# Attention, layers and dispatch of a fused network, from two stages to one written-out stage of 78 beats

## The chip, the cores and the metric

One core of a Trainium2 chip (trn2) runs the whole network in one launch. The metric is the device time of that launch in microseconds (us); less is better. The engines are TensorE (PE, with its weight loads shown as PEld), VectorE (DVE), ScalarE (ACT), GpSimd (POOL) and the DMA queues, which SyncE (SP) mostly feeds.

## The reference, cut to what matters

Input and output are 8 images of 128 channels and 32x32 pixels, 8192 tokens of 128 numbers in all, in float32. Three residual steps follow each other:

```python
x = x + _L0_conv_ref(_gn(x), ...)              # group norm, deformable convolution
t = _to_tokens(x)
t = t + _L1_attn_ref(_ln_t(t), ...)            # token norm, attention layer
t = t + _L1_ffn_ref(_ln_t(t), ...)             # token norm, top-2 of 8 experts
```

The second one is what the change touches, with the router of the third:

```python
res = _local_rel_attention(x, ...)             # 8 heads, 65 keys around each token, bias by distance
xs = _layer_norm(x + res, ln1_g, ln1_b)
res = relu(xs @ W_lin + b_lin)
xs = _layer_norm(xs + res, ln2_g, ln2_b)       # added to t
logits = xt @ Wr + br                          # xt: the normed tokens; softmax, top 2, weights
```

Every token then goes to its two experts; their weighted sum is added to t.

## The kernel before, in words

Tokens lie as channels by tokens: `X` holds the residual stream, `XA` the normed tokens with 32 zero columns at either end of an image. A **half** is half an image, 512 tokens or four **tiles** of 128; there are 16. `program` calls stages, each a block of its own with a barrier behind it: `front` and `sample_fast` (convolution), `token_norm`, `attention`, `finish` (layers and dispatch), `experts`, `combine`. In each block every engine has its own written list, and semaphores order them.

**`attention`** works in 64 units of 128 tokens, four to a half; a Fori loop (L1187) holds four halves and runs three times, so it returns twice; the two halves before it and the two behind it are written out. For a unit: PE's `scores` (L1304, 32 small matmuls into `p_s`, four banks), DVE's `soft` (L1480 adds scaled scores and bias table, L1486 the row maximum), ACT's `exps` (L1407, eight heads), PE's `turn` (L1317, eight transposes into `p_t`), `copy_pt` (ACT L1415, DVE L1493), PE's `mix` (L1331, weights by values into `p_o`), DVE's `scale` (reciprocal L1501, multiply L1503), PE's `turn_out` (L1340) and ACT's `copy_out` (L1419). PE's body of unit t is, in order:

```python
scores(t + 1); turn_out(t - 2); product; turn(t); product; mix(t - 1)
```

The products make queries and keys (L1273), values (L1279) and the output projection (L1284) a half at a time through one bank, `p_m`; ACT or DVE drains each (L1401, L1458, L1464, L1471), and the next waits for that. DVE also copies `XA` into a ring `XS` for the values (L1449). SP moves the values' windows (12 transfers a half).

**`finish`** starts behind attention's barrier and goes over the halves in steps of a skewed pipeline: centering 1 (PE L1747), square (ACT L1800), variance 1 (L1756), inverse root (ACT Ln and Exp L1792, L1794), DVE's multiply L1972, the linear layer (L1738), ReLU (ACT L1833), residual (DVE L1965), centering 2 (L1762), variance 2 (L1732), DVE L1957 and L1961 (sum into `X`). Their PSUM banks are the stage's own. Halves then go in groups to dispatch (half 0, six pairs, the last three one by one): transposes (L1706), router matmuls (L1714), DVE's statistics (`note`, L1861 to L1869) and choice (`choose`, L1876 to L1903), counts by PE (L1721, L1722), DVE's `place_rows` (L1910 to L1950), the normed rows by ACT (L1813), and POOL's indirect DMAs that write each tile's rows twice to the experts' table in DRAM (L1690, behind a counter step L1686). At the end DVE makes the table of blocks (L1989 to L2018) and folds the experts' input scale into `w1` (L2023), and SP writes the padding rows.

Of the kernel before, what the change touches and what calls it, by code (L numbers as in the profile page):

```python
# [14 lines left out]
ALU = mybir.AluOpType  # L15
# [31 lines left out]
PADS = EXPERTS + SPARE  # L47
ROW = P + 4
# [878 lines left out]

class MidWeights:
# [16 lines left out]
    MID, EXP = 16 * 10, 16 * 6  # L945
# [12 lines left out]
def token_norm(nc, d, X, XA, const, mid, ew):  # L958
# [4 lines left out]
    with ExitStack() as st:  # L963
# [11 lines left out]
        written = sem(nc, st, "n_written")  # L975

        with nc.Block() as block:
            @block.sync
            def _(sp):
                for dst, src in ((center, "c_center"), (ones, "c_ones"), (const.ident, "c_ident")):  # L980
                    sp.dma_start(dst[:], d[src]).then_inc(w_in, 16)

# [5 lines left out]
                for dst, src in ((ew.w1, "w1"), (ew.w2, "w2"), (ew.lng, "ln_g"), (ew.lnb, "ln_b"), (ew.b1, "b1")):  # L988
                    sp.dma_start(dst[:], d[src]).then_inc(mid.experts_in, 16)
# [59 lines left out]
def attention(nc, d, XA, const):  # L1049
# [7 lines left out]
    PADA = PIX + 2 * REACH  # L1057
    VW = DV + 1
    NU = TOK // (UB * QB)
    NS = 2 * IMAGES  # L1060
    US = NU // NS
    NB = US * UB
    NT = HEADS
    NPM = 1
    COPIES = 12
    with ExitStack() as st:
        ident = const.ident
        wq = sb(nc, st, "a_wq", [P, 2, P])
        wk = sb(nc, st, "a_wk", [P, 2, P])
        wv = sb(nc, st, "a_wv", [P, P])  # L1070
        wo = sb(nc, st, "a_wo", [P, P])
        bq = sb(nc, st, "a_bq", [P, 2])
        bk = sb(nc, st, "a_bk", [P, 2])
        bv = sb(nc, st, "a_bv", [P, P])
        bo = sb(nc, st, "a_bo", [P, 1])


        bias = [sb(nc, st, f"a_bias{v}", [P, 4, 2, QW]) for v in range(3)]
        XS = [sb(nc, st, f"a_XS{j}", [P, CH]) for j in range(2)]
        Q = [sb(nc, st, f"a_Q{j}", [P, 2, CH]) for j in range(2)]  # L1080
        KT = [sb(nc, st, f"a_KT{j}", [P, 2, PADA]) for j in range(2)]

        VT = [sb(nc, st, f"a_VT{j}", [P, TPC, HEADS, VW]) for j in range(2)]
        V = sb(nc, st, "a_V", [QW, 2 * NB, HEADS, VW])
        E = [sb(nc, st, f"a_E{b}", [P, NT, QW]) for b in range(2)]
        PT = [sb(nc, st, f"a_PT{b}", [QW, NT, P]) for b in range(2)]
        nm = sb(nc, st, "a_nm", [P, 2, NT])
        rsum = sb(nc, st, "a_rsum", [P, 2, HEADS])
        O = [sb(nc, st, f"a_O{b}", [P, P]) for b in range(2)]
        OT = [sb(nc, st, f"a_OT{j}", [P, CH]) for j in range(2)]  # L1090

        p_s = ps(nc, st, "a_ps", (P, 4, CH))
        p_t = ps(nc, st, "a_pt", (P, 2, NT // 2, P))
        p_m = [ps(nc, st, f"a_pm{k}") for k in range(NPM)]
        p_o = ps(nc, st, "a_po")
        toeplitz = nc.dram_tensor("toeplitz", [QB, 4, 2, QW], F32, kind="Internal").ap()

        w_in = sem(nc, st, "a_w_in")
        rel_in = sem(nc, st, "a_rel_in")
        masked = sem(nc, st, "a_masked")  # L1100
        cleared = sem(nc, st, "a_cleared")
        staged = sem(nc, st, "a_staged")
        windowed = sem(nc, st, "a_windowed")
        made = sem(nc, st, "a_made")
        act_took = sem(nc, st, "a_act_took")
        dve_took = sem(nc, st, "a_dve_took")
# [1275 lines left out]
```

## Time and profile before

| | us |
|---|---|
| runs of the kernel | 1542.88, 1550.11, 1549.81 (median 1549.81) |
| the profiled execution: span | 1543.9 |
| front and sampling, 0 to 543.7 | 543.7 |
| token norm, 543.7 to 597.4 | 53.7 |
| attention, 597.4 to 991.4 | 394.0 |
| layers and dispatch, 991.4 to 1218.1 | 226.7 |
| experts and combine, 1218.1 to the end | 325.8 |

The profiled execution is one of its own; what is known of its time is its span, from the first to the last instruction. Over that span PE is busy 1234.7 us, PE's weight loads 794.5, DVE 980.6, ACT 777.2 and POOL 607.0; the mean granted clock of PE is 0.889 of full speed. The stage bounds are the first instructions behind each barrier. These totals mix stages with different limits: the stage views further down tell more than they do. In a row of a timeline stand the start, the duration, the engine, the line, the operation with what it writes and reads, how many instructions the row holds, and in brackets the idle time before it and what ended it.

### The profile page before, as it was taken

The page shows a single profiled execution, that of the slowest core. Times are in us where ns is not written, and L with a number is a line of the kernel's source. Part 1 is how long each engine was busy: PE and PEld are TensorE (multiplying, and loading weights), DVE is VectorE, ACT ScalarE, POOL GpSimd, SP SyncE. Part 2 cuts the span into 40 slices and gives each one's busy share as a digit, 9 for nine tenths or more (in the row PEclk, how much of TensorE's full clock was granted, in tenths as well). Part 3 has the DMA queues.
Part 4 walks back from the last instruction along what each step waited for, and adds up shares of the span by engine and source line. Part 5 has one row for each costly group of instructions (what it writes and reads, how often), then busy time and mean ns, then how long its engine had stood idle before and what let it go on. Part 6 is the DMA issues. An engine that isn't in the chain of part 4 may idle for free. (4 is left out here: it accounts for less than half of the span.)

```text
span 1543.9 us, 42335 instructions
## 1 busy us (share of the span) xinstructions
PE 1234.7 (80%) x13479; PEld 794.5 (51%) x13480; DVE 980.6 (64%) x2321; ACT 777.2 (50%) x2037; POOL 607.0 (39%) x681
## 2 busy tenths in 40 slices
PE   3981799999999965788888788787865399999974
PEld 1551344444444421455555555433334399999962
DVE  4996888888888511566566566467765244444435
ACT  1212545555455243456565555467752277777750
POOL 2000577878778800000000000015777455656550
PEclk9995899999999987799899999698865699999985
DMA  3000000000000030111211211101111122222228
GB/s 120 0 0 12 1 1 1 0 0 0 0 0 0 1 138 27 45 36 35 46 40 31 46 44 36 57 9 37 54 51 63 44 68 67 69 67 67 69 68 306
DMA packets 69491, 67.75 MB, mean 44 GB/s; under 512 B 13151, under 2 KB 59231, under 8 KB 68983
## 3 DMA queue, kind: packets, MB, share of 16 engines
q1 hardware_dynamic: 58615, 44.23, 10.5%
q0 software_dynamic: 8448, 17.58, 3.4%
q10 hardware_dynamic: 2304, 4.20, 0.7%
q8 instruction: 90, 1.47, 0.4%
q14 instruction: 34, 0.28, 0.1%
HBM read 29.93 MB, written 23.00 MB: 34 GB/s over the span
## 5 line engine op out<-in xcount | busy, mean ns | idle before, releaser
L2157 ACT ACTIVATE e_hT<-e_ph,e_b 128x128 f32<-128x128 f32 x544 | 155.0, 368 | 73.7 <-PE e_ph L2114 68.5
L1407 ACT ACTIVATE a_E<-a_E,a_nm 128x96 f32<-128x96 f32 x512 | 142.7, 362 | 72.1 <-DVE a_nm L1486 72.0
L440 POOL TENSOR_TENSOR s_pc<-s_wide,VP 128x512 f32<-128x512 f32 x112 | 143.1, 1278 | 74.7 <-ACT s_wide L519 68.6
L673 PE MATMUL s_pbc<-s_AT,s_sel 120*128 120x512 bf16 x400 | 134.5, 386 | 32.8 <-ACT s_wide L519 17.5
L431 POOL TENSOR_TENSOR s_acc<-s_acc,s_pb 128x512 f32<-128x512 f32 x112 | 142.3, 1270 | 22.0 <-DVE s_pb L602 21.5
L684 PE MATMUL s_pout<-s_pa,s_opT 128*128 128x512 f32 x288 | 150.8, 605 | 0.0
L2125 PE MATMUL e_py<-e_w,e_hT 128*128 x1088 | 149.3, 280 | 1.3 <-ACT e_hT L2157 0.8
L1674 POOL MEMSET m_total<- 128x8 f32 x1 | 0.1, 109 | 378.5 <-POOLq L1193 378.5
L2114 PE MATMUL e_ph<-e_xT,e_w1s 128*128 128x128 f32 x1088 | 147.3, 279 | 0.3 <-DVE e_w1s L2186 0.2
L1690 POOL DMA_INDIRECT slots<-m_pay,m_pos x128 | 129.2, 1009 | 38.5 <-issue 37.6
L2095 POOL DMA_INDIRECT picks<-e_yw,e_rows x136 | 134.6, 990 | 22.6 <-POOL e_tick L2093 18.5
L2114 PEld LDWEIGHTS e_ph<-e_xT,e_w1s 128*128 128x128 f32 x1088 | 133.8, 194 | 2.0 <-issue 1.0
L2125 PEld LDWEIGHTS e_py<-e_w,e_hT 128*128 128x128 f32 x1088 | 131.8, 191 | 4.6 <-issue 3.0
L519 ACT ACTIVATE s_wide<-s_pbc 128x512 f32<-128x512 f32 x112 | 66.4, 593 | 115.7 <-PE s_pbc L673 113.7
L602 DVE TENSOR_TENSOR s_pb<-s_pbc,VP 128x512 f32<-128x512 f32 x144 | 98.1, 681 | 27.8 <-PE s_pbc L673 27.8
L689 PE MATMUL s_pout<-s_pc,s_opT 128*128 128x512 f32 x224 | 114.4, 592 | 0.0
L673 PEld LDWEIGHTS s_pbc<-s_AT,s_sel 120*128 120x128 bf16 x400 | 38.4, 98 | 132.3 <-issue 56.7
L602 DVE TENSOR_TENSOR s_pa<-s_pbc,VP 128x512 f32<-128x512 f32 x144 | 98.3, 683 | 12.4 <-PE s_pbc L673 11.8
L2186 DVE COPY e_w1s<-e_w 128x512 f32 x136 | 59.0, 434 | 67.6 <-issue 67.6
L1304 PE MATMUL a_ps<-a_KT,a_Q 32*32 32x96 f32 x4096 | 67.5, 262 | 30.6 <-issue 27.2
L1480 DVE SCALAR_TENSOR_TENSOR a_E<-a_ps,a_bias 128x768 f32<-128x768 f32 x64 | 61.1, 955 | 45.1 <-PE a_ps L1304 44.6
L2192 DVE TENSOR_TENSOR e_yb<-e_py,e_b 128x128 f32<-128x128 f32 x136 | 39.6, 291 | 74.3 <-PE e_py L2125 74.0
(221 smaller groups left out, 2426.9 us busy)
## 6 DMA issues: line engine op xcount, KB each, us to landing
a_V<-a_VT SPq DMA_DIRECT2D x176, 68.0 KB
e_rows<-slots SPq DMA_DIRECT2D x136, 66.0 KB, 1.8
c_y<-picks SPq DMA_DIRECT2D x16, 512.0 KB, 6.1
X<-in_x SPq DMA_DIRECT2D x8, 512.0 KB, 8.5
e_w<-in_w SPq DMA_DIRECT2D x2, 2048.0 KB, 10.1
out<-c_o ACTq DMA_DIRECT2D x16, 256.0 KB
picks<-e_yw,e_rows POOLq DMA_INDIRECT x136, 2.3
slots<-m_pay,m_pos POOLq DMA_INDIRECT x128, 2.3
```

The costliest lines, as they stand in the source:

```text
L431: nc.gpsimd.tensor_tensor(acc[j][:], before, prod_b[b % 3][:], ALU.add)\
L440: nc.gpsimd.tensor_tensor(prod_c[k][:].rearrange("p (a b) -> p a b", a=HALF), wide[k][:].rearrange("p (a b) -> p a b", a=HALF), window(n, ...
L602: dve.tensor_tensor(out[:].rearrange("p (a b) -> p a b", a=HALF), p_bc[bank_of["spread", t]][:].rearrange("p (a b) -> p a b", a=HALF), win ...
L673: pe.matmul(p_bc[bank_of["spread", t]][:], sel[:, t % 5, :], AT[j][:, t // 5, :], start=True, stop=True).then_inc(bc, 1)
L684: pe.matmul(p_out[j][:], opT[:], prod_a[a % 3][:], start=(a == 0), stop=False)\
L689: pe.matmul(p_out[j][:], opT[:], prod_c[(j * NC + i) % 2][:], start=False, stop=False)\
L1407: act.activation(E[u % 2][:, o, :], E[u % 2][:, o, :], ACT.Exp, bias=nm[:, u % 2, o:o + 1]).then_inc(powered, 1)
L1690: nc.gpsimd.indirect_dma_start(out=slots, out_offset=bass.IndirectOffsetOnAxis(ap=pos[h][:, c, t:t + 1].bitcast(U32), axis=0), in_=pay[c][ ...
L2095: nc.gpsimd.indirect_dma_start(out=picks, out_offset=bass.IndirectOffsetOnAxis(ap=rows[j][:, P:P + 1].bitcast(U32), axis=0), in_=yw[j][:], ...
L2114: last = pe.matmul(p_h[j % 2][:, q * P:(q + 1) * P], w1s[j % 2][:, q, :], xT[j % 2][:], start=True, stop=True)
L2125: last = pe.matmul(p_y[j % 2][:, 0:P], hT[j % 2][:, q, :], w2[:, bass.ds(e, 1), q * P:(q + 1) * P].rearrange("p o h -> p (o h)"), start=(q ...
L2157: ins = act.activation(hT[j % 2][:, q, :], p_h[j % 2][:, q * P:(q + 1) * P], ACT.Gelu, bias=b1[:, bass.ds(e, 1), q:q + 1].rearrange("p o h ...
```

## The change

`attention` and `finish` become one function, `middle`, with one block and no loop: 78 **beats** (64 units and 14 more), all written out. The weights and the bias table of attention are loaded in `token_norm`'s block. A beat t is a unit as before, with one step of the layers of some half put in behind `turn`. Half h has its centering 1 in beat t = 7 + 4h, variance 1 one beat later, then the linear layer, centering 2, variance 2, the sum into `X`, the transposes (beat + 6) and the router (beat + 8); so each beat works at one to three of them. Their results go into the score banks `p_s`, as PSUM has no others: the layer matmul waits until DVE has read the scores (`biased`), and the next scores wait until ACT or DVE has read the layer's result (`emptied`). ACT does its layer step between the fourth and fifth exponential, and the inverse roots behind its copy. What DVE multiplied in L1957 and L1972, and the normed rows that ACT made, POOL makes now. Groups of halves are as before (0; 1 and 2; ... 11 and 12; 13; 14; 15); the dispatch of one is spread over five to eight beats, and of the last three over fewer. The ring `XS` and its copies go; `w2` of the experts shares its memory with the keys, and loads when the last scores are done. The padding rows go from DRAM to DRAM. The matmuls that fold the experts' bias move from behind the last half into beat 68. The new functions of PE, POOL and DVE are, in the diff cut to its core:

```diff
+def middle(nc, d, X, XA, const, aw, mid, ew, table, slots):
...
+    C1, V1, LIN, C2, V2, ADD, TURN, JUDGE = 0, 1, 2, 3, 4, 5, 6, 8
+    BEATS = NU + 14
...
+                sp.wait_ge(scored, NU)
+                sp.dma_start(ew.w2, d["w2"]).then_inc(w2_in, 16)
...
+                def rows(g, first):
...
+                        nc.gpsimd.tensor_scalar(pay[0][h][:, k, 0:P], pay[0][h][:, k, 0:P], inv[h][:, 1, k:k + 1],
+                                                nb[h][:, k:k + 1], ALU.mult, ALU.add).then_inc(paid, 1)
...
+                for t in range(BEATS):
+                    h = at(t, LIN)
+                    if h is not None:
+                        pool.wait_ge(inverted1, h * 2 + 2)
+                        pool.wait_ge(kept1, h + 1)
+                        if h:
+                            pool.wait_ge(added, h)
+                        nc.gpsimd.tensor_tensor(xs[:], c1g[:], sq1[:], ALU.mult).then_inc(scaled1, 1)
+                    h = at(t, ADD)
+                    if h is not None:
+                        pool.wait_ge(inverted2, h * 2 + 2)
+                        pool.wait_ge(kept2, h + 1)
+                        if h:
+                            pool.wait_ge(finished, h)
+                        nc.gpsimd.tensor_tensor(z[:], c2g[:], sq2[:], ALU.mult).then_inc(scaled2, 1)
+                    g = group_at(t, ORDER)
+                    if g is not None:
+                        rows(g, 0)
+                    g = group_at(t, COUNT)
+                    if g is not None and tiles(g) > TPC:
+                        rows(g, TPC)
+                    for part in range(4):
+                        g = group_at(t - part, WRITE)
+                        if g is not None and PARTS[g][-1] < NS - 3:
+                            send(g, part, 4)
+                    g = group_at(t, WRITE)
+                    if g is not None and PARTS[g][-1] >= NS - 3:
+                        send(g, 0, 1)
...
+                def emptied(t):
+                    h = at(t, C1)
+                    if h is not None:
+                        pe.wait_ge(kept1, h + 1)
+                    h = at(t, V1)
+                    if h is not None:
+                        pe.wait_ge(inverted1, h * 2 + 1)
...
+                def scores(t):
...
+                    if t:
+                        pe.wait_ge(biased, t)
+                    emptied(t - 2)
...
+                def layers(t):
+                    if t + 1 < NU:
+                        pe.wait_ge(biased, t + 2)
+                    else:
+                        emptied(t - 1)
+                    h = at(t, V1)
+                    if h is not None:
+                        pe.wait_ge(squared1, h + 1)
+                        pe.matmul(p_s[:, 0], ones[:], sq1[:], start=True, stop=True).then_inc(varied1, 1)
+                    h = at(t, LIN)
+                    if h is not None:
+                        pe.wait_ge(scaled1, h + 1)
+                        pe.matmul(p_s[:, 0], lin[:], xs[:], start=True, stop=True).then_inc(layered, 1)
...
+                for t in range(BEATS):
+                    if t + 1 < NU:
+                        scores(t + 1)
+                    if 0 <= t - 2 < NU:
+                        turn_out(t - 2)
+                    for x in due(t)[:1]:
+                        product(x)
+                    if t < NU:
+                        turn(t)
+                    layers(t)
+                    for x in due(t)[1:]:
+                        product(x)
+                    if 0 <= t - 1 < NU:
+                        mix(t - 1)
+                    if t == NU + 4:
...
+                        exps(t + 1, 0, HEADS // 2)
+                    layers(t)
+                    if t + 1 < NU:
+                        exps(t + 1, HEADS // 2, HEADS)
+                    if t < NU:
+                        copy_pt(t)
+                    roots(t)
...
+                    if t + 1 < NU:
+                        soft(t + 1)
...
+                    if 0 <= t - 1 < NU:
+                        scale(t - 1)
+                    g = group_at(t, PLACE)
+                    if g is not None:
+                        place(g)
+                    g = group_at(t, CHOOSE)
                     if g is not None:
                         choose(g)
+                    g = group_at(t, ORDER)
                     if g is not None:
+                        mark(g)
...
-            attention(nc, d, XA, const)
...
-            finish(nc, d, X, XA, const, mid, ew, table, slots)
+            middle(nc, d, X, XA, const, aw, mid, ew, table, slots)
```

Three places of the programs' order follow, without time. The names: `a_` are tiles and semaphores of attention, `l_` of the layers, `m_` of dispatch; `e_shared` holds the keys in the changed kernel.

**PE, in the layers and dispatch stage of the kernel before**: one step and the start of the next, with a group's counts and the first transposes of the next group.

```order
L1738 MATMUL l_pl<-l_xs0,l_lin 128x512 [waits l_clipped,l_scaled0]
L1721 MATMUL m_pr<-m_both,m_upper 128x32 [waits m_route]
L1722 MATMUL m_pr<-m_both,m_full 128x32
L1747 MATMUL l_pc10<-XA,k_center 128x512 [waits l_scaled0]
L1756 MATMUL l_pv<-l_sq11,k_ones 128x512 [waits l_inverted1,l_inverted0,l_squared0]
L1762 MATMUL l_pc2<-l_y1,k_center 128x512 [waits l_scaled1,l_added]
L1706 MATMUL m_pt0<-k_ident,X 128x128 [waits m_paid,l_finished]
L1706 MATMUL m_pt0<-k_ident,X 128x128 x3
L1706 MATMUL m_pt1<-k_ident,X 128x128 x4
L1714 MATMUL m_pr<-m_wrc,X 128x8 [waits m_route]
```

Layer matmuls wait for layer and dispatch results alone and write banks of that stage. **PE in the changed kernel, in the stage of units**: the last beat of a half, from the output's transpose to the next scores.

```order
L1526 MATMUL a_po<-k_ident,a_O1 128x128 [waits a_ostored,a_scaled]
L1499 MATMUL a_pt<-k_ident,a_E1 96x128 [waits a_pt_dve,a_powered]
L1499 MATMUL a_pt<-k_ident,a_E1 96x128 [waits a_powered] x3
L1499 MATMUL a_pt<-k_ident,a_E1 96x128 [waits a_pt_act,a_powered]
L1499 MATMUL a_pt<-k_ident,a_E1 96x128 [waits a_powered] x3
L1555 MATMUL a_ps<-XA,k_center 128x512 [waits a_dve_took,a_biased]
L1559 MATMUL a_ps<-l_sq2,k_ones 128x512 [waits l_squared2]
L1564 MATMUL a_ps<-m_wrc,X 128x8 [waits l_finished]
L1564 MATMUL a_ps<-m_wrc,X 128x8 x3
L1517 MATMUL a_po<-a_V,a_PT0 32x17 [waits a_ostored,a_scaled,a_windowed1,a_pt_act,a_pt_dve]
L1517 MATMUL a_po<-a_V,a_PT0 32x17 x31
L1486 MATMUL a_ps<-e_shared,a_Q0 32x96 [waits l_inverted2,m_fetched,l_kept1,a_biased]
```

The centering of one half (L1555), the variance (L1559) and the router (L1564) of earlier ones stand now between a unit's transposes (L1499) and its mix (L1517), and write the banks of the scores; the scores that follow (L1486) wait for four semaphores, three of them of the layers and dispatch.

**DVE, at the end of a group's placing, before**: behind it come the next group's statistics and four layer steps.

```order
L1939 TENSOR_REDUCE m_fpos<-m_wpos 128x8 [waits m_route]
L1944 COPY m_pay<-m_dest 128x8 [waits m_sent0]
L1944 COPY m_pay<-m_dest 128x8
L1946 COPY m_pay<-m_sm 128x8
L1947 TENSOR_TENSOR m_pay<-m_sm,m_ex 128x8
L1950 CAST m_pos<-m_fpos 128x16 [waits m_route]
L1861 BN_STATS m_stats<-m_pt 128x6 [waits m_turned]
L1861 BN_STATS m_stats<-m_pt 128x6 x3
L1861 BN_STATS m_stats<-m_pt 128x6 [waits m_turned]
L1861 BN_STATS m_stats<-m_pt 128x6 x3
L1957 SCALAR_TENSOR_TENSOR l_z<-l_pc,l_vec,l_sq 128x512 [waits l_inverted1]
L1961 SCALAR_TENSOR_TENSOR X<-l_z,l_vec,X 128x512 [waits l_scaled1]
```

The bias step is not in this list: attention's DVE list was over. **DVE in the changed kernel, the same place**: the end of placing (L1901 to L1912) and what follows.

```order
L1901 TENSOR_REDUCE m_fpos<-m_wpos 128x8 [waits m_route]
L1906 COPY m_pay<-m_dest 128x8 x2
L1908 COPY m_pay<-m_sm 128x8
L1909 TENSOR_TENSOR m_pay<-m_sm,m_ex 128x8
L1912 CAST m_pos<-m_fpos 128x16 [waits m_route]
L1762 SCALAR_TENSOR_TENSOR a_E<-a_ps,a_bias 128x768 [waits a_turned,a_scored]
L1768 TENSOR_REDUCE a_nm<-a_E 128x8 [waits a_biased]
L1799 SCALAR_TENSOR_TENSOR X<-l_z,l_vec,X 128x512 [waits l_scaled2]
L1775 COPY a_PT<-a_pt 96x512 [waits a_mixed,a_turned]
L1742 TENSOR_SCALAR e_shared<-a_pm,a_bk 128x512 [waits a_made]
L1783 RECIPROCAL a_rsum<-a_po 128x8 [waits a_oturned,a_mixed]
L1785 TENSOR_TENSOR a_O<-a_po,a_rsum 128x128 [waits a_scaled]
```

The bias step of the next unit's scores (L1762) now stands right behind the placing, and what waits for the scores' banks stands behind both. Two of the layer steps are gone from DVE's list.

**POOL, at the end of dispatch, before**: the last groups' transfers and the end of its list.

```order
L1690 DMA slots<-m_pay,m_pos 67584x132 x16
L1686 TENSOR_TENSOR m_tick<-m_tick 1x1 [waits m_paid,m_labelled,m_ticked]
L1690 DMA slots<-m_pay,m_pos 67584x132 x16
L1686 TENSOR_TENSOR m_tick<-m_tick 1x1 [waits m_paid,m_labelled,m_ticked]
L1690 DMA slots<-m_pay,m_pos 67584x132 x8
L1656 UNCONDITIONAL_BRANCH [waits m_sent1,m_sent0]
```

The list then only waits for the transfers to land. **POOL in the changed kernel**, ahead of the last three groups: a half's second multiply, the first four of a group's 16 transfers, a half's first multiply, and the first two row scalings of the next group.

```order
L1405 TENSOR_TENSOR l_z<-l_c2g,l_sq 128x512 [waits l_finished,l_kept2,l_inverted2]
L1382 TENSOR_TENSOR m_tick<-m_tick 1x1 [waits m_paid,m_labelled,m_ticked]
L1386 DMA slots<-m_pay,m_pos 67584x132 x4
L1398 TENSOR_TENSOR l_xs<-l_c1g,l_sq 128x512 [waits l_added,l_kept1,l_inverted1]
L1370 TENSOR_SCALAR m_pay<-m_pay,m_inv,m_nb 128x128 [waits m_sent1,m_rooted,m_shifted]
L1372 TENSOR_SCALAR m_pay<-m_pay,m_inv,m_nb 128x128
```

Multiplies (L1398, L1405) and row scalings (L1370, L1372) now stand between transfers in one list, and a group's 16 transfers come as one part of four in a beat and the rest behind the next work.

## Rows read from the trace of the kernel before

**Rows 1.** Windows: us; busy PE, PEld, DVE, ACT, POOL (instructions); clock; DMA; GB/s.

```profile
624.00:991.40 367.40, 304.80 (x9036) 206.05 (x9036) 233.69 (x394) 207.70 (x670) 0.00 (x0) 0.91 0.17 38
991.40:1218.10 226.70, 146.26 (x456) 80.12 (x456) 136.52 (x730) 118.87 (x268) 131.73 (x143) 0.73 0.15 48
```

**Rows 2.** Timeline, one attention beat with two products.

```profile
802.98 1.12 PE L1284 MATMUL a_pm<-a_OT,a_wo 128*128 128x512 f32 x2
...
804.04 0.74 PE L1331 MATMUL a_po<-a_V,a_PT 96*32 96x17 f32 x64
...
804.76 1.04 PE L1304 MATMUL a_ps<-a_KT,a_Q 32*32 32x96 f32 x64
...
805.79 0.29 DVE L1503 TENSOR_TENSOR a_O<-a_po,a_rsum 128x128 f32<-128x128 f32 x1
806.01 0.96 DVE L1480 SCALAR_TENSOR_TENSOR a_E<-a_ps,a_bias 128x768 f32<-128x768 f32 x1
...
806.13 0.33 PE L1340 MATMUL a_po<-k_ident,a_O 128*128 128x128 f32 x1 [0.33 <-DVE a_O L1503]
...
806.33 1.34 PE L1317 MATMUL a_pt<-k_ident,a_E 128*96 128x128 f32 x8
...
807.99 2.23 ACT L1407 ACTIVATE a_E<-a_E,a_nm 128x96 f32<-128x96 f32 x8 [1.21 <-DVE a_nm L1486]
```

**Rows 3.** Waits, 620 to 985: us in all, times, longest.

```profile
DVE a_E L1480 <- PE a_ps L1304: 44.6, 39, 4.4
...
PE a_ps L1304 <- issue: 27.2, 17, 3.9
```

**Rows 4.** Timeline, attention's first product, and bias steps of units 9 and 64.

```profile
603.61 2.07 PE L1273 MATMUL a_pm<-XA,a_wq 128*128 128x512 f32 x2 [8.69 <-DMA a_bv<-in_bv]
...
667.58 0.96 DVE L1480 SCALAR_TENSOR_TENSOR a_E<-a_ps,a_bias 128x768 f32<-128x768 f32 x1
...
978.61 0.96 DVE L1480 SCALAR_TENSOR_TENSOR a_E<-a_ps,a_bias 128x768 f32<-128x768 f32 x1 [0.52 <-PE a_ps L1304]
```

**Rows 5.** Timeline, a layer step on DVE and on ACT.

```profile
1008.72 0.75 DVE L1965 SCALAR_TENSOR_TENSOR l_y<-l_y,l_vec,l_xs 128x512 f32<-128x512 f32 x1 [1.94 <-ACT l_y L1833]
1008.86 0.60 ACT L1800 ACTIVATE l_sq<-l_pc 128x512 f32<-128x512 f32 x1 [0.17 <-PE l_pc L1747]
...
1009.72 0.69 ACT L1792 ACTIVATE l_sq<-l_pv,k_eps 128x512 f32<-128x512 f32 x1 [0.26 <-PE l_pv L1756]
```

**Rows 6.** Timeline, DVE, dispatch of eight tiles: placing, statistics, choosing, marking.

```profile
1091.76 0.16 DVE L1914 TENSOR_SCALAR m_sm<-m_ex 128x8 f32<-128x8 f32 x1
...
1095.45 1.67 DVE L1861 BATCH_NORM_STATS2 m_stats<-m_pt 128x6 f32<-128x128 f32 x8
1097.15 0.64 DVE L1865 BATCH_NORM_AGGREGATE m_mv<-m_stats 128x2 f32<-128x6 f32 x8
...
1100.99 0.17 DVE L1876 SCALAR_TENSOR_TENSOR m_nb<-m_mv,m_inv 128x8 f32<-128x8 f32 x1
...
1102.26 0.17 DVE L1891 TENSOR_TENSOR m_dif<-m_top 128x8 f32<-128x8 f32 x1
...
1104.17 0.23 DVE L1903 TENSOR_TENSOR m_both<-m_hot 128x64 f32<-128x64 f32 x1
```

**Rows 7.** Timeline, PE, scores that waited for issue.

```profile
649.76 0.73 PE L1304 MATMUL a_ps<-a_KT,a_Q 32*32 32x96 f32 x37 [2.37 <-issue]
...
765.26 1.30 PE L1304 MATMUL a_ps<-a_KT,a_Q 32*32 32x96 f32 x64 [3.90 <-issue]
```

**Rows 8.** Costliest groups (page), POOL's multiply of 512 columns.

```profile
L440 POOL TENSOR_TENSOR s_pc<-s_wide,VP 128x512 f32<-128x512 f32 x112 | 143.1, 1278 | 74.7 <-ACT s_wide L519 68.6
```

**Rows 9.** Timeline, POOL, the end of dispatch and the experts' start.

```profile
1204.19 0.18 POOL L1686 TENSOR_TENSOR m_tick<-m_tick 1x1 f32<-1x1 f32 x1
...
1213.40 0.95 POOL L1690 DMA_INDIRECT slots<-m_pay,m_pos  x1 [0.30 <-issue]
1218.13 0.09 POOL L2086 MEMSET e_tick<- 1x2 f32 x1 [3.78 <-POOLq L1656]
```

More of the change, by code:

```diff
@@ L47 @@
 PADS = EXPERTS + SPARE
+PADA = PIX + 2 * REACH
 ROW = P + 4
@@ L1645, in finish, with tile, tokens @@
         ticked = sem(nc, st, "m_ticked")
[L1647 to L1654 removed]
+        started = sem(nc, st, "m_started")
+        def tile(h, k):
+            a = h * CH + k * P
+            return X[:, a:a + P]
+        def tokens(h):
+            n, hf = divmod(h, 2)
+            return XA[:, n, REACH + hf * CH:REACH + (hf + 1) * CH]
         with nc.Block() as block:
@@ new lines, in turn @@
+                def turn(t):
+                    for b in range(2):
+                        for k in range(HEADS // 2):
+                            o = b * (HEADS // 2) + k
+                            pe.wait_ge(powered, t * HEADS + o + 1)
+                            if k == 0 and t:
+                                pe.wait_ge((pt_dve, pt_act)[b], t)
+                            last = pe.transpose(p_t[0:QW, b, k, :], E[t % 2][:, o, :], ident[:])
+                        last.then_inc(turned, 1)
@@ L1818, in step, with take, exps @@
-                def step(s):
-                    k = s % 2
-                    g = group(s, 2)
+                act.wait_ge(bias_out, 1)
+                def take(x):
+                    _, m, s = x
+                    act.wait_ge(made, number[x] + 1)
+                    act.activation(Q[s % 2][:, m, :], p_m[:], ACT.Identity, bias=bq[:, m:m + 1])\
+                       .then_inc(act_took, 1)
+                def exps(t, lo, hi):
+                    act.wait_ge(maxed, t + 1)
+                    for o in range(lo, hi):
+                        act.activation(E[t % 2][:, o, :], E[t % 2][:, o, :], ACT.Exp,
+                                       bias=nm[:, t % 2, o:o + 1]).then_inc(powered, 1)
@@ L1834, in step @@
-                    if within(s):
-                        square(s, 0, p_c1[k], sq1[k])
-                    if within(s - 1):
-                        invert(s - 1, 0, sq1[1 - k])
-                    if within(s - 3):
-                        square(s - 3, 1, p_c2, sq2[1 - k])
-                    g = group(s, 1)
-                    if g is not None:
-                        rows_out(g)
-                for s in range(STEPS):
-                    step(s)
+                        act.activation(ex[:, 0:n], dif[:, 0:n], ACT.Exp).then_inc(power, 1)
```

1159 lines of the change are left out of this document (524 added, 635 removed).

## The prediction, made before the changed kernel was run

> **What bounds the kernel now.** I read the time by stages first, then one beat of attention, then the durations of the layer and dispatch work, then POOL. The stage table [rows 1] shows attention (597.4 to 991.4, of which 367.4 us hold the 64 units) and, strictly behind it, layers and dispatch, 226.7 us, before the experts start at 1218.1. In attention TensorE (PE) is busy 304.8 of 367.4 us, ScalarE (ACT) 207.7, VectorE (DVE) 233.7 and GpSimd (POOL) nothing; in layers and dispatch PE has 146.3 of 226.7, DVE 136.5, ACT 118.9. Neither stage fills an engine, so laying one over the other can gain at most what the busiest engine leaves free: PE's two sums are 451 us of 594, so no more than some 143 us. What remains of it is decided by the chain within a beat.
>
> One beat [rows 2]: scores for the next unit take 1.04, DVE's bias step starts 1.25 after the scores' start and lasts 0.96, ACT's eight exponentials start 1.98 after the bias step, and PE meanwhile does the output transpose (0.33), eight transposes (1.34), products (1.12 each) and the mix (0.74). A beat with two products sums to 1.04+0.33+2.24+1.34+0.74 = 5.69 on PE, so PE sets the beat now. PE also stands still without a semaphore: 27.2 us before the scores in 17 waits put down to issue [rows 3].
>
> **The change, part by part.** Program order shows that it does interleave: each layer matmul stands between the transposes and the mix of a unit, so the rival that nothing moves has no chance.
>
> *Start.* The attention weights (8 loads), the bias table's 7 transfers and POOL's two copies go into the token norm, whose block runs from 543.7 to 597.4 on other engines' work; I price them at nothing, and if that cover failed they cost at most the 6.2 us they cost now: PE's first product waits until 603.61 [rows 4] for the bv load. Left at the start are a dozen small memsets and two bias matmuls, some 2.7 us from 597.4: the units begin 3.5 earlier. The 16 DVE copies of XA go too; they lay in DVE's slack.
>
> *Beats 0 to 6* have no layer work: as now. The ninth unit's bias step moves from 667.58 [rows 4] to 664.1, so beat 7 starts (1.25 before) at 662.8.
>
> *Beats 7 to 63.* Layer results sit in the score banks, so a beat is now a ring: scores, bias step, layer matmul (not before the bias step ends), ACT's reading of it (after four of eight exponentials), next scores. PE's own path, per place u in a half, from [rows 2]:
> u=0 (variance 1): 1.04+0.33+1.12+1.34+1.12+1.12+0.74 = 6.81.
> u=1 (linear, four transposes at half of 1.34): 7.48.
> u=2 (centering 2): 6.81.
> u=3 (centering 1, variance 2, router matmuls, these taken like four transposes; no product): 6.36.
> ACT's path: 1.25+1.98+1.12 = 4.35, then Ln 0.69, or Relu and a copy (0.69 and a Square's 0.60) 1.29, or Square and a copy 1.20, or these and Ln 1.89 [rows 5]: 5.04, 5.64, 5.55, 6.24. All shorter than PE's.
> DVE is the third path. Its placing, choosing and marking stand behind the scaling, which waits for the mix at the beat's end, and ahead of the next bias step. The scaling ends about 0.6 into the next beat when nothing else stands before it (at 1.3 behind two drains, 806.08 [rows 2]), so 0.65 is free. Placing eight tiles takes 3.7 (1091.76 to 1095.45), choosing and marking 3.4 (1100.99 to 1104.40), which I split into 1.3 and 2.1; statistics of four tiles 0.83, of the second half of a group 1.67 with aggregation [rows 6]; the residual step 0.75 [rows 5]. So once in 8 beats each:
> after placing, u=0 has its bias step at 4.3; 4.3+0.96+1.12+1.12+0.74 = 8.24.
> after choosing, u=1 has it at 1.95; hidden, 1.95+1.98+1.12+1.29 = 6.3 is under 7.48.
> after marking and the residual step, u=2 has it at 3.45; soft ends 5.38, key copy 6.13, output product and mix: 7.99.
> u=3 behind statistics: bias step at 1.48 or 2.27, ACT's path 6.47 or 7.26.
> Sum over two halves: 6.81+8.24+7.48+7.48+6.81+7.99+6.47+7.26 = 58.5, or 7.32 a beat.
>
> *Instruction supply.* Of the 27.2 us, two waits of 3.9 stand at a loop's return, one of them at 765.26 [rows 7]. They go with the loop. The rest is 19.4/64 = 0.3 a beat, and it also occurs in code without a loop: 2.37 us at 649.76, in the halves that are written out [rows 7]. I keep 0.3, ends 0 (PE waits there anyway) and 0.45. The Trainium skill (Runtime: NRT & Kernel Launch, Instruction fetch mechanics) says the sequencer fetches ahead in sequence, so that a page boundary is mostly hidden and only a taken branch stalls it. By that rule the beat would be 7.35; the row at 649.76 differs, and the measurement is kept in the sum.
>
> *Clock.* Attention ran at a mean granted clock of 0.91 [rows 1] and its beats came to 5.66 (55 of them from 667.58 to 978.61 [rows 4]). My sum for them is 5.13, three with two products and one with none of four (3 x 5.69 and 3.45), and 5.55 with the issue waits, 27.2/64. So dips cost 0.1 there. I add 0.03: more of the new beat's time is waiting for ACT and DVE, where a slower PE costs nothing. Beat: 7.65. Beat 64 starts at 662.8 + 57 x 7.65 = 1098.9.
>
> *POOL beside the beats.* Two multiplies of 512 columns a half at 1.28, sixteen transfers a group at 1.25, 16 row scalings a group [rows 8, 9]. No row shows a scaling of 128 columns; the ends are the one-element add, 0.18, and the 512-column multiply, 1.28; on the line between them 0.45. In 8 beats that is 5.1+20+7.2 = 32 of 61 us, or 46 at the upper end: hidden either way. xs comes 1.3 after the inverse root and is there when the transposes end, with 0.5 to spare; if POOL were still issuing transfers, each late one costs 1.25 on PE.
>
> *SP.* The 192 window transfers stay, with longer beats to land in; w2 (2 MB) loads once the last scores are done, beside the tail, and the eight spare pads go first: nothing.
>
> *Tail.* Half 15 needs 14 more beats without units. PE's 64 bias-fold matmuls sit inside, but POOL ends last: from about 14.3 into the tail (last mix, output product, centering, variance, roots of half 14) its queue holds 3 multiplies, 24 scalings, 40 transfers and four counter steps: 3.8+10.8+50+0.7 = 65.3. Then 3.8 to the experts, as now (the idle time before 1218.13 [rows 9]). Ends for the scalings give -6 and +20. In all 83.4.
>
> **Sum.** 1098.9+83.4 = 1182.3 against 1218.1: 35.8 less. The profiled execution then spans 1543.9-35.8 = 1508.1; it lies 5.9 under the median of the runs, 1549.8, so on that scale **1514 us**, 2.3% faster. Half a per cent, 7.7 us, is about what a measurement tells from no change.
>
> **Rivals.**
> *The ring opens wider* (beats on PE's path alone, 6.87+0.3 = 7.17): needs DVE's dispatch to fall into its idle time after all. For it: DVE waits 44.6 us for scores now [rows 3]. Against: program order puts it ahead of the bias step. 57 x 0.48 = 27 less: 1487. Chance 0.10.
> *Written-out code is not starved* (beats 0.3 shorter): in the loop half of the longest waits are at returns; against it is the row at 649.76. 1514-17 = 1497. Chance 0.13. The Trainium skill's Runtime page, named above, is its rule.
> *Hand-offs cost more* than the rows show: each beat has two more crossings between engines; a further 0.65 a beat uses up the gain, 1551. For it: now every such crossing is hidden behind PE. Chance 0.09.
> *Slower: the clock.* PE waits in the ring, is granted 1.2 GHz, and the next beat is PE-bound at that rate. A product at 1.2 GHz takes 2.07 [rows 4] against 1.12, so PE's path of 6.87 becomes about 11. The gain is gone when a beat in five runs so (0.19 x 3.35 = 0.63 a beat, 36 us over 57); at a third of the beats the time is 1514+57 x 1.06 = 1574. For it: layers and dispatch had 0.73 [rows 1]. Against: PE's path fills 6.87 of 7.65 in my beat, 90%, and filled 5.13 of 5.66, 91%, in attention, which had 0.91. The Trainium skill (TensorE: Matmul & The Clock Gate, What's actually happening) says that throttled is the default and activity releases it; the two stage rows agree. Chance 0.16.
>
> **How the numbers follow.** Forecast 0.52 (1489 to 1540: beat 7.2 to 8.1). Faster by over 0.5% are the forecast and the first two rivals, 0.75; within it the hand-offs, 0.09; slower the clock, 0.16. For the range I take the fetch case and most of the open ring below, POOL's and the fetch's upper ends and the hand-offs above: 1475 to 1556, which leaves out the clock at its price and a little below.
>
> **What would show it.** Right: units from about 620; beats of 5.6 until the first layer matmul, then 7.3 to 8.0, longest behind placing and marking, with DVE's dispatch rows directly ahead of late bias steps; layer ACT rows done before PE asks for the bank at u=0 to 2; experts starting near 1182, POOL's transfers last. Wrong: granted clock under 0.85 in the stage, PE waiting for ACT in every beat, POOL late with xs, or a start after 1218.

## The result and the profile after

The changed kernel takes **1475.76 us** (median of four runs, 1473.08 to 1483.07) against 1549.96 before: the ratio is 0.9542, interval 0.9517 to 0.9568. The forecast was 1514; the direction was right and the time lies at the lower edge of the range, so the gain was twice the forecast's. The profiled execution took 1483.07, the longest of the four; its span is 1481.3.

| us, profiled executions | before | after |
|---|---|---|
| start of the attention block | 597.4 | 596.0 |
| ninth bias step | 667.58 [rows 4] | 658.31 |
| last (64th) bias step | 978.61 [rows 4] | 1040.19 |
| experts start | 1218.13 [rows 9] | 1157.54 |
| from there to the end | 325.8 | 323.8 |

The two bias steps:

```profile
658.31 0.96 DVE L1762 SCALAR_TENSOR_TENSOR a_E<-a_ps,a_bias 128x768 f32<-128x768 f32 x1 [0.41 <-PE a_ps L1486]
...
1040.19 0.96 DVE L1762 SCALAR_TENSOR_TENSOR a_E<-a_ps,a_bias 128x768 f32<-128x768 f32 x1
```

By windows (columns as in [rows 1]) the units with the layers in them, the tail, and the experts:

```profile
617.60:1046.00 428.40, 364.01 (x9210) 239.40 (x9210) 313.45 (x846) 283.52 (x822) 157.58 (x206) 0.95 0.19 49
1046.00:1157.54 111.54, 44.24 (x282) 32.54 (x282) 49.50 (x276) 17.09 (x39) 70.74 (x94) 0.55 0.13 39
1157.54:1481.30 323.76, 290.41 (x2376) 278.57 (x2376) 148.58 (x440) 196.31 (x681) 159.26 (x273) 0.91 0.31 95
```

PE is busy 364 of 428 us at a mean granted clock of 0.95, where attention alone had 0.91 and layers and dispatch 0.73 [rows 1]. In the tail it is busy 44 of 112 at 0.55, near the lower level of 1.2 GHz. What PE waits for while the units run (614 to 1046; us in all, times, longest):

```profile
PE a_ps L1537 <- DVE a_E L1762: 16.7, 6, 3.5
...
PE a_ps L1486 <- issue: 8.8, 11, 1.8
...
PE a_ps L1551 <- DVE a_E L1762: 7.4, 6, 1.4
...
PE a_ps L1486 <- ACT l_sq L1680: 6.5, 10, 1.3
PE a_ps L1555 <- DVE a_E L1762: 5.5, 8, 1.2
...
PE a_po L1526 <- issue: 2.9, 2, 1.8
...
PE a_ps L1541 <- POOL l_xs L1398: 1.0, 2, 0.6
```

The first and the longest kind is the layer matmul that waits for DVE's bias step; L1537 is variance 1, the matmul of the beat behind placing. The waits for issue before the scores, 27.2 before [rows 3], are down to 8.8, and with the smaller kinds to 12.6. Now the same beat as in [rows 2], PE's list in a beat with two products and a layer matmul, from one unit's scores to the next:

```profile
879.94 0.95 PE L1486 MATMUL a_ps<-e_shared,a_Q 32*32 32x96 f32 x64 [0.58 <-ACT l_sq L1680]
...
880.82 0.33 PE L1526 MATMUL a_po<-k_ident,a_O 128*128 128x128 f32 x1
...
880.98 1.02 PE L1433 MATMUL a_pm<-XA,a_wq 128*128 128x512 f32 x2
...
881.84 1.04 PE L1499 MATMUL a_pt<-k_ident,a_E 128*96 128x128 f32 x8
...
882.72 1.02 PE L1537 MATMUL a_ps<-l_sq,k_ones 128*128 128x512 f32 x2
...
883.58 1.02 PE L1433 MATMUL a_pm<-XA,a_wk 128*128 128x512 f32 x2
...
884.53 0.74 PE L1517 MATMUL a_po<-a_V,a_PT 96*32 96x17 f32 x64
...
885.20 0.96 PE L1486 MATMUL a_ps<-e_shared,a_Q 32*32 32x96 f32 x64
```

The durations sum to 0.95+0.33+1.02+1.04+1.02+1.02+0.74 = 6.12, but the starts lie 0.88, 0.16, 0.86, 0.88, 0.86, 0.95 and 0.67 apart, **5.26** in all: each row's end reaches into the next row. And a beat behind the placing:

```profile
909.28 0.95 PE L1486 MATMUL a_ps<-e_shared,a_Q 32*32 32x96 f32 x64
...
909.82 0.16 DVE L1876 TENSOR_SCALAR m_sm<-m_ex 128x8 f32<-128x8 f32 x1
...
914.29 0.17 DVE L1912 CAST m_pos<-m_fpos 128x16 int32<-128x16 f32 x1
...
914.37 0.95 DVE L1762 SCALAR_TENSOR_TENSOR a_E<-a_ps,a_bias 128x768 f32<-128x768 f32 x1
...
915.37 2.08 PE L1537 MATMUL a_ps<-l_sq,k_ones 128*128 128x512 f32 x2 [3.14 <-DVE a_E L1762]
```

The scores are written by 910.2; DVE places from 909.82 to 914.46, its bias step comes at 914.37 and not near 910.5, and PE stands 3.14 us before the variance matmul, which then runs at half rate, 2.08 (granted clock 0.50). The beats of the units by their place among eight, from the starts of their scores (units 9 to 62, six or seven of each; the forecast's own sum in the first column, without its 0.33 for issue and clock):

```
t mod 8                     forecast  after   e2    e4    e6    e8
0  variance 1                   6.81   5.20  6.48  5.21  5.20  5.20
1  linear, behind choosing      7.48   6.79  7.41  6.69  7.53  6.13
2  centering 2, marking         7.99   7.44  7.39  6.34  7.39  6.97
3  centering 1, variance 2      6.47   7.01  7.19  6.44  6.84  6.68
4  variance 1, behind placing   8.24   8.64  8.01  5.29  7.09  5.29
5  linear                       7.48   6.20  6.52  7.36  7.09  6.53
6  centering 2                  6.81   6.45  6.84  6.55  6.21  6.54
7  as 3, with aggregation       7.26   7.60  7.71  7.51  7.27  6.65
sum                            58.54  55.33 57.55 51.39 54.62 49.99
```

The seven beats of place 4 hold one ahead of the first placing, of 5.26; the six behind a placing take 7.56 to 10.79, 9.20 in the mean. How far executions differ by themselves is told by e3, whose edit does nothing before the tail: its column would have 6.50 in place 3, 8.37 in place 4 and a sum of 54.37. Differences of 0.5 in a place, or 1 in a sum, say nothing.

The tail, on POOL, ACT and PE:

```profile
1057.83 0.44 POOL L1370 TENSOR_SCALAR m_pay<-m_pay,m_inv,m_nb 128x128 f32<-128x128 f32 x1
...
1095.40 0.95 POOL L1386 DMA_INDIRECT slots<-m_pay,m_pos  x1 [0.30 <-issue]
...
1097.75 0.60 ACT L1661 ACTIVATE m_pay<-a_ps 128x512 f32<-128x512 f32 x1 [14.85 <-DMA slots<-m_pay,m_pos]
...
1098.44 2.04 PE L1551 MATMUL a_ps<-l_y,k_center 128*128 128x512 f32 x2 [15.41 <-ACT m_pay L1661]
...
1105.30 1.26 POOL L1405 TENSOR_TENSOR l_z<-l_c2g,l_sq 128x512 f32<-128x512 f32 x1 [8.95 <-ACT l_sq L1691]
...
1119.23 0.96 POOL L1386 DMA_INDIRECT slots<-m_pay,m_pos  x1 [0.30 <-issue]
...
1121.58 0.60 ACT L1661 ACTIVATE m_pay<-a_ps 128x512 f32<-128x512 f32 x1 [16.03 <-DMA slots<-m_pay,m_pos]
...
1157.54 0.09 POOL L2057 MEMSET e_tick<- 1x2 f32 x1 [3.18 <-POOLq L1307]
```

ACT lifts half 14's transposed tokens (L1661) into a payload tile at 1097.75 after 14.85 us of waiting for transfers of two groups before, the last of which POOL had issued at 1095.40. PE's centering of half 15 waits for that lift (15.41, its bank is next), and POOL then for a result of that chain (8.95). Half 15's lift waits again, 16.03, for transfers that POOL issues up to 1119.23.

### The profile page after: what moved, and what is told of

Same layout as the page of the kernel before. It is cut to its first block and busy times, and to the rows that moved or that the text cites. A ratio compares the mean times of both kernels' runs of the same rounds, so it can differ in the third digit from the quotient of the medians.

```text
span 1481.3 us, 41520 instructions
## 1 busy us (share of the span) xinstructions
PE 1193.9 (81%) x13483; PEld 782.1 (53%) x13484; DVE 974.0 (66%) x2318; ACT 753.3 (51%) x1960; POOL 703.6 (48%) x842
## 5 line engine op out<-in xcount | busy, mean ns | idle before, releaser
L1627 ACT ACTIVATE a_E<-a_E,a_nm 128x96 f32<-128x96 f32 x512 | 148.5, 364 | 117.8 <-DVE a_nm L1768 117.3
L2096 PE MATMUL e_py<-e_shared,e_hT 128*128 x1088 | 150.4, 281 | 1.1 <-ACT e_hT L2128 1.1
L2096 PEld LDWEIGHTS e_py<-e_shared,e_hT 128*128 128x128 f32 x1088 | 132.7, 192 | 4.6 <-issue 2.9
L1405 POOL TENSOR_TENSOR l_z<-l_c2g,l_sq 128x512 f32<-128x512 f32 x16 | 20.3, 1269 | 165.1 <-ACT l_sq L1691 165.1
L1486 PE MATMUL a_ps<-e_shared,a_Q 32*32 32x96 f32 x4096 | 70.3, 259 | 23.0 <-issue 8.8
L1762 DVE SCALAR_TENSOR_TENSOR a_E<-a_ps,a_bias 128x768 f32<-128x768 f32 x64 | 61.0, 954 | 28.7 <-PE a_ps L1486 28.5
```

Source lines behind the costliest of these rows:

```text
L1627: act.activation(E[t % 2][:, o, :], E[t % 2][:, o, :], ACT.Exp, bias=nm[:, t % 2, o:o + 1]).then_inc(powered, 1)
L2096: last = pe.matmul(p_y[j % 2][:, 0:P], hT[j % 2][:, q, :], w2[:, bass.ds(e, 1), q * P:(q + 1) * P].rearrange("p o h -> p (o h)"), start=(q ...
```

## The experiments

e1 to e4 and e6 are the changed kernel with one edit, e5 is the kernel before with one, e7 and e8 put several together. Before was timed beside all of them (medians 1546.6), and the ratios are to that; "us less" and "us more" are differences of medians to the change's 1475.76, whose own before had 1549.96, so some 3 us of each are uncertain by that alone.

**e1: the layers behind the units.** How much of the gain is the written-out units, and how long is a beat without layers?

```diff
+    LAG = NU - 7
-        h, odd = divmod(t - 7 - back, US)
+        h, odd = divmod(t - 7 - LAG - back, US)
```

(and the same LAG in the dispatch beats)

> The layers' beats are moved back by 57, so that the 64 units run written out but alone and the layers and dispatch come behind them in the same stage. Theory 1 (the beat is the ring of the score banks: PE's own list, counted from start to start of its rows, is 5.26 in a beat with two products and a layer matmul; what it is longer is DVE's dispatch ahead of the bias step): without layers the units take 5.0 to 5.3 a beat, against 5.66 in the loop of the kernel before, since fewer waits for issue are left; the layers alone then take some 4.3 us a beat, 135 beats in all, and the time is 1600 to 1650 us. Theory 2 (the forecast's count of PE's list was right, and the units gained from something else in the written-out code): the units alone take 5.6 to 5.7 a beat, as before.

One run took 1669.91 us. Its rows: bias steps 9 and 64, the window of the units, and PE's waits for issue from 615 to 950.

```profile
659.86 0.96 DVE L1763 SCALAR_TENSOR_TENSOR a_E<-a_ps,a_bias 128x768 f32<-128x768 f32 x1 [0.35 <-PE a_ps L1487]
...
943.11 0.96 DVE L1763 SCALAR_TENSOR_TENSOR a_E<-a_ps,a_bias 128x768 f32<-128x768 f32 x1 [0.34 <-PE a_ps L1487]
```

```profile
659.00:945.00 286.00, 240.50 (x7841) 166.51 (x7829) 202.12 (x330) 180.22 (x577) 0.00 (x0) 0.97 0.19 44
```

```profile
PE a_ps L1487 <- issue: 28.3, 22, 2.3
...
PE a_pm L1441 <- issue: 9.2, 12, 0.9
```

A beat is (943.11-659.86)/55 = 5.15, as theory 1 said, against 5.66 before; the layers alone then cost 400 us (expected 4.3 a beat, measured some 5.6), so that the time lies above the 1600 to 1650 that theory 1 gave. The waits for issue are the surprise: 28.3 us before the scores alone, without any loop. So writing out did not do away with them; with the layers in the beats there are 8.8, and what covers or spares the others wasn't tried. The Trainium skill (Runtime: NRT & Kernel Launch, Instruction fetch mechanics) says that crossing a boundary of its 16 KiB code blocks is mostly hidden, and that a taken branch can stall. If fetching is what these waits are, the rows don't agree; that it is, no run here shows.

**e2: all eight exponentials ahead of ACT's layer step.**

```diff
-                    layers(t)
                     if t + 1 < NU:
                         exps(t + 1, HEADS // 2, HEADS)
+                    layers(t)
```

> ACT makes all eight exponentials before its layer step, where the changed kernel puts the step between the fourth and the fifth. Theory 1 (ring): next scores wait 1.17 longer for the bank in each beat where ACT's reading is near the end of the ring; 0.6 to 1.1 more in each of 57 beats, 35 to 60 us: 1510 to 1535 us. Theory 2 (PE's own list of 6.8 to 7.5 a beat hides ACT's path, as forecast): no more than 5 us, 1472 to 1482.

Measured 1493.35 (0.9666, 0.9633 to 0.9698), 18 us more than the change. The direction is theory 1's, the size less than half of it: 0.28 a beat. From 614 to 1046 PE waits 56 us for ACT before the scores, where the changed kernel has 12. The table tells where: place 0, whose bias step is on time and whose PE list is 5.26, grew by 1.28 (5.20 to 6.48), the place behind placing not at all. That ACT's path has 1.2 us and more to spare behind PE's at u=0 to 2, as forecast, falls.

**e3: payload tiles of their own for the last two groups** (tiles that long free groups had used).

```diff
+    def spot(g):
+        return (g % 2, 0) if g < GRP - 2 else [(1, TPC), (0, 0)][g - GRP + 2]
-                        act.activation(pay[0][g % 2][:, q:q + TPC, 0:P],
+                        act.activation(pay[0][m][:, o + q:o + q + TPC, 0:P],
```

> The last two groups write their payload into tiles that have long been free, so that ACT's lift of halves 14 and 15 no longer waits for the transfers of the group two before. Theory 1 (the tail is the layers' chain held up by the payload ring: ACT waits 14.9 and 16.0 us there): the experts start some 15 to 22 us earlier, 1454 to 1461 us. Theory 2 (POOL's 40 transfers, 24 scalings and 3 multiplies fill the tail, as forecast): POOL's list only closes up, 5 us or less, 1471 to 1476.

Measured 1462.56 (0.9468, 0.9437 to 0.9499), 13 us less. The lifts of halves 14 and 15 wait for no transfer now:

```profile
1071.56 0.60 ACT L1680 ACTIVATE m_pay<-a_ps 128x512 f32<-128x512 f32 x1 [0.17 <-PE a_ps L1562]
...
1090.87 0.60 ACT L1680 ACTIVATE m_pay<-a_ps 128x512 f32<-128x512 f32 x1 [13.33 <-PE a_ps L1562]
```

The second waits 13.33 for PE, whose transposes wait for POOL's multiply, which stands behind transfers. From the last bias step to the experts the tail is 1133.87-1031.36 = 102.5 against 117.4. So 15 of the tail were the payload ring, at the lower end of theory 1 (the time lies between the two theories). Then POOL's list is the bound, as forecast: from 1062.4 to 1130.1 it never stands idle for more than 0.31.

**e4: DVE's dispatch where DVE waits.** Two thirds of the placing ahead of the fetch of the router's result, the marking ahead of the values' drain, for groups 0 to 5.

```diff
+                    if g is not None and g < GRP - 4:
+                        place(g, 0)
                     h = judged_at(t)
                     if h is not None:
                         fetch(h)
...
+                        mark(g)
                     for x in due(t)[1:]:
                         take(x)
```

> For groups 0 to 5 the first two thirds of DVE's placing stand ahead of its fetch of the router's result, where DVE waits for PE now, the rest stays at the beat's end, and the marking stands ahead of the drain of the values. Theory 1 (what stands ahead of the bias step at a beat's end lengthens the next beat nearly one for one): 3.7 us become 1.4 and 2.1 become 0 there, 2 to 3 us less in each of six groups, 1458 to 1466 us. Theory 2 (DVE is late wherever the work stands, as the fetch, the drains and the scaling behind it hold up PE instead): within 4 us of 1476.

Measured 1451.56 (0.9420, 0.9369 to 0.9470), 24 us less by the medians and 19 by the two ratios: the upper end of theory 1 or above it. In its trace placing runs from 886.35, behind the copy of the transposes:

```profile
886.35 0.16 DVE L1882 TENSOR_SCALAR m_sm<-m_ex 128x8 f32<-128x8 f32 x1
...
888.56 0.18 DVE L1824 COPY m_LR<-a_ps 128x32 f32<-128x32 f32 x1
...
888.93 0.95 PE L1486 MATMUL a_ps<-e_shared,a_Q 32*32 32x96 f32 x64 [0.58 <-DVE m_LR L1824]
...
890.37 0.95 DVE L1762 SCALAR_TENSOR_TENSOR a_E<-a_ps,a_bias 128x768 f32<-128x768 f32 x1
...
891.71 1.02 PE L1537 MATMUL a_ps<-l_sq,k_ones 128*128 128x512 f32 x2
```

The fetch comes at 888.56, PE's scores wait 0.58 for it, and the variance matmul that had waited 3.14 waits for nothing. Place 4 goes from 8.64 to 5.29, the six beats behind a placing from 9.20 to 5.30, PE's own list. Place 5 grew, from 6.20 to 7.36: PE's linear matmul now waits for POOL's multiply, 8.4 us in six waits (614 to 1016). The units also run at a higher clock:

```profile
655.00:1016.00 361.00, 318.84 (x8198) 214.30 (x8185) 278.45 (x806) 258.36 (x742) 160.52 (x206) 0.99 0.21 54
```

**e5: the kernel before with its loop written out.**

```diff
-            with eng.Fori(0, (NS - 4) // 4) as i:
-                for k in range(4):
-                    body(i * 4 + (k + 2), (k + 2) % 4, i * 2 + (k + 2) // 2)
+            for s in range(2, NS - 2):
+                body(s, s % 4)
```

> The kernel before, with its loop over groups of four halves written out in all engines and nothing else changed. Theory 1 (a good part of the gain is the loop's going: in e1 the units alone came to 5.15 a beat against 5.66): 55 beats by 0.3 to 0.5 less, 16 to 27 us: 1519 to 1531 us. Theory 2 (only the two returns of 3.9 us go, other waits for issue stay, and the rest of e1's 0.5 is the changed order of products and drains): 5 to 10 us less, 1537 to 1542.

Measured 1536.32 (0.9936, 0.9913 to 0.9958): 10 us, theory 2. Of the change's 74 us no more than that is the loop. The window of the loop, and PE's waits of the units, 618 to 975:

```profile
672.00:945.00 273.00, 218.57 (x6926) 146.13 (x6925) 179.21 (x303) 159.22 (x514) 0.00 (x0) 0.97 0.18 40
```

```profile
PE a_ps L1303 <- issue: 26.1, 21, 2.4
...
PE a_po L1330 <- DMA a_V<-a_VT: 10.8, 10, 2.5
...
PE a_pm L1272 <- DVE a_KT L1457: 7.2, 12, 0.8
PE a_pm L1283 <- DVE a_VT L1463: 6.4, 13, 0.7
PE a_po L1339 <- DVE a_O L1502: 5.9, 19, 0.6
...
PE a_po L1330 <- issue: 5.5, 9, 1.2
```

The same window of the kernel before:

```profile
672.00:945.00 273.00, 229.15 (x6668) 153.96 (x6666) 175.29 (x296) 154.46 (x496) 0.00 (x0) 0.93 0.17 39
```

The two returns are gone, yet the waits for issue before the scores are 26.1 in place of 27.2, and before the mix 5.5 in place of 1.0: new ones took their place. The clock in that window went from 0.93 to 0.97, and the beats from 5.66 to 5.52. From there to e1's 5.15 are another 20 us in 55 beats, which neither the loop nor the layers explain. PE's waits for other engines and transfers sum to some 35 us here (the four largest are shown) and to 6 in e1 (615 to 950), so the changed kernel's order of a unit's work has removed most of them; which of its moves did was not tried.

**e6: POOL's two multiplies back on DVE.**

```diff
-                        nc.gpsimd.tensor_tensor(xs[:], c1g[:], sq1[:], ALU.mult).then_inc(scaled1, 1)
+                        dve.tensor_tensor(xs[:], c1g[:], sq1[:], ALU.mult).then_inc(scaled1, 1)
```

(and z likewise)

> The two multiplies of 512 columns a half go from POOL back to DVE, behind the bias step of their beats. Theory 1 (DVE's list is what a beat waits for): 1.5 us more of DVE work in four beats, of which half or more lengthens them, 10 to 25 us: 1486 to 1501. Theory 2 (POOL's multiplies hold up DVE's own instructions, rows of 1.0 to 1.3 in place of 0.2 beside them, and hand the result over late): no loss or a gain, 1466 to 1478.

Measured 1478.73 (0.9568, 0.9536 to 0.9601): no difference that these intervals can tell from the change, so theory 1 falls. The table shows two effects that cancel: the linear beats (1 and 5) grow by 0.7 and 0.9, as PE's linear matmul now waits for DVE's multiply (16.4 us in 13 waits, 614 to 1046), and place 4, behind placing, shrinks from 8.64 to 7.09. Why POOL's multiply costs there stands in the last section.

**e7 and e8: together.** e7 is e3 and e4 with a group's transfers cut 3, 5, 4, 4; e8 adds three moves.

```diff
+                    cut = (0, 3 * n // 8, n, 3 * n // 2, 2 * n) if parts == 4 else (0, 2 * n)
...
+                    if h is not None and late:
+                        note(h)
                     h = judged_at(t)
...
+                        choose(g)
                         mark(g)
...
-                    if t == NU + 4:
+                    if t == BEATS - 1:
```

> e3 and e4 in one kernel, and a group's 16 transfers cut into 3, 5, 4 and 4 in place of 4 times 4, so that POOL comes in time to the multiply before the linear layer (PE waited 1.55 us for it in e4). If the three lie on different paths they add: 13 + 24 + about 5 less than 1476, 1429 to 1440 us. If e3's gain was that of the same waits as e4's, 1445 to 1452.

> e7 with three more moves: the statistics of a group's second half from ahead of the bias step to ahead of the fetch, the choice next to the marking, and PE's 64 bias-fold matmuls to the last beat. Theory 1 (DVE work ahead of the bias step is paid in full, work beside PE's wait is free): 1.5 and 1.1 less in each of six groups, and 2 in the tail: 15 to 18 us less than e7. Theory 2 (the moved steps only shift the lateness into drains and scaling): within 4 us of e7.

e7 took 1436.12 (0.9291, 0.9262 to 0.9320): the parts add. e8 took **1427.52** (0.9242, 0.9209 to 0.9276), 8.6 less than e7, about half of what theory 1 gave it: against e7's own beats (6.74, 6.36 and 7.48 in places 1, 2 and 7), place 7 shrank by 0.8 and place 1 by 0.6, but place 2 grew by 0.6, for a reason that was not traced; none of the three is far above the scatter. It beats both kernels. Its units:

```profile
655.00:1008.00 353.00, 319.63 (x8290) 214.57 (x8291) 277.50 (x801) 261.34 (x751) 159.98 (x205) 1.00 0.22 56
```

PE is busy 320 of 353 us at full clock; a sum of 49.99 for eight beats stands against an estimated 43 for PE's list alone (twice the 21.7 of the next section).

## Why the prediction was right, and where it was off

In the profile the experts start at 1157.5 where 1182.3 was forecast, 24.8 earlier: 5.8 before beat 7, 39 in the beats, and 20 given back in the tail. That the time lies in the range, by 0.8 us at its lower edge, is luck: it lies outside 1489 to 1540, which had the chance of 0.52, the beat of 6.94 is below even the open ring's 7.17, and without the tail's 20 it would have left the range. What was right is that laying the layers over the units gains, and that DVE's dispatch ahead of the bias step makes the longest beats.

**Start: under-estimated.** Forecast 3.5 earlier, measured 9.3 (667.58 to 658.31): 1.4 stand ahead of the stage, the bias step of the first unit moved 6.4 (625.82 to 619.38), as the whole wait for the bv load went, and the eight beats behind it took 38.9 in place of 41.8.

**PE's path: the term that failed.** "PE's own path, per place u", 6.81, 7.48, 6.81 and 6.36, was a sum of durations. By starts u=0 is 5.26, as seven beats of the changed kernel in which PE waits for nothing show; the other three, priced by the same distances, are an estimate of 5.7, 5.4 and 5.3: some 21.7 for a half and not 27.5. It is a little low: the shortest beats without an idle PE are 5.91 at u=1 and, in e4, 5.76 at u=2. In [rows 2] the same can be seen: the mix starts 1.06 behind a product of 1.12, and the scores 0.72 behind a mix of 0.74. And the eight transposes' 1.34 there is not their price (0.88 here). That the sum gave 5.69 and the beat 5.66 was a coincidence: with 5.26-0.86 = 4.4 for PE's list in a beat with two products, some 1.3 of the beat before were waits for other engines, waits for issue and a lower clock. So "PE sets the beat now" fell too, and with it the reading that ACT's path is hidden (e2).

**DVE's lateness: the right mechanism, its size partly by luck.** Behind placing the bias step was forecast at 4.3 and the beat at 8.24. In the six such beats the step comes at 3.70 (half 0, four tiles) and at 4.54 to 5.08, and the beat takes 9.20 in the mean. Two terms that the sum didn't have made up for PE's list, which is priced too high in the same 8.24: POOL's multiply stretches one DVE row (last section), and in three of the six PE, after waits of 2.6 to 3.1, works at a mean granted clock of 0.75 to 0.83. e4 takes away the lateness and the beat becomes PE's list. Behind marking 7.99 was forecast and six beats took 7.68; for statistics 6.47 and 7.26 against 7.01 and 7.60. With PE's path shorter this is the bound of more beats than the forecast had, and the rival of a wider open ring, "DVE's dispatch to fall into its idle time", is what e4 had to make by hand.

**Issue and clock: not to be told apart from the lists.** 0.33 a beat stood for them. The measured beats contain their waits for issue (12.6 us in 64 units, 0.2 a beat) and every dip of the clock, and still sum to 0.40 a beat less than the engines' lists were given ((58.54-55.33)/8); the 0.33 make the rest of 7.65 against 6.94. How much of the 0.2 lengthens a beat the runs don't show. "It also occurs in code without a loop" was right, more than expected (e1, e5), and the rival that written-out code is not starved fell. The clock rival fell as a whole, as the granted clock rose to 0.95, and to 0.99 and 1.00 as e4 and e8 took PE's waits away; in the three beats behind a placing its mechanism shows.

**POOL: right in its own times.** A scaling of 128 columns takes 0.44 (forecast 0.45), and the multiply came late for PE in two beats, 1.0 us in all; that it would be late behind transfers came true in e4. What it does to DVE's rows was not in the sum.

**Tail: mis-sized.** The sum let POOL's list run closed up, 65.3, which left out that its own input waits for ACT, and ACT for POOL's earlier transfers: from the last bias step 117.4, where the forecast's numbers give 97.5 (1182.3-1084.8). e3 takes 15 of these 20 away.

**Scale.** The forecast added 5.9 to go from the profiled span to the median; this span lies 5.5 above its median (1481.3 against 1475.76). With 2.0 less from the experts' start to the end, that is 13 of the 38 between forecast and result.

## What to carry to other kernels

Price an engine's list from start to start of its rows, in a stretch where it waits for nothing, not by its durations. In a ring of in-order engines a burst of small instructions is paid in full when it stands ahead of the step that the ring waits for, and is nearly free a few instructions on, where its engine waits anyway: look for that place before splitting or moving work to another engine. A buffer ring that is long enough in the steady state can be the bound of the tail, where nothing else covers its wait.

## What was not expected of the hardware

Some DVE instructions that begin while POOL multiplies 512 columns last until POOL has ended. The second row lies in a placing, beside the first; the third is the same instruction without POOL beside it:

```profile
852.25 1.27 POOL L1405 TENSOR_TENSOR l_z<-l_c2g,l_sq 128x512 f32<-128x512 f32 x1 [13.28 <-ACT l_sq L1691]
...
852.35 1.25 DVE L1896 TENSOR_TENSOR m_rank<-m_rank,m_cnt 128x64 f32<-128x64 f32 x1
...
1069.26 0.23 DVE L1896 TENSOR_TENSOR m_rank<-m_rank,m_cnt 128x64 f32<-128x64 f32 x1
```

POOL's ends at 853.52, DVE's at 853.60: 1.25 in place of 0.23. In the changed kernel thirteen DVE rows are about 1 us longer in this way: one in each of eight placings, beside z's multiply, and five in choosings, beside xs's; in e6 there is none. Others that begin beside such a multiply are not held: a MAX8 (L1843) takes 0.15, the fetch of the router's result from PSUM (L1824) 0.19. The Trainium skill (SBUF — State Buffer, Who interferes with whom) says that a DVE instruction with two SBUF inputs contends with a GpSimd instruction that reads SBUF, and calls the lock exclusive; the rows shown agree. Four of the thirteen, three copies and a scaling, have one SBUF input, which that sentence does not cover.

In the six beats behind a placing these rows are 5.8 us longer in all, 0.8 of the 1.55 that place 4 lost in e6 in the mean of its seven beats. Most of the rest is the clock: three of the six have a mean granted clock of 0.82, 0.75 and 0.83 in the changed kernel and 1.00 in e6, where PE's wait ahead of them is 1.0 to 1.6 us shorter.

The waits for issue before the scores came to less with the layers in the beats (28.3 us in e1, 8.8 in the changed kernel, with the same instructions in both). It is not that PE's waits for DVE's bias step cover them: in e8, where the layer matmuls wait 1.3 us for it in place of 32 (614 to 1008), they are 8.4. What decides when they occur stays open.
